# A two-layer expert FFN with modulated LayerNorm on one core: group sums kept in SBUF, x loaded three items ahead, y accumulated onto a negative mean, and 1/std as a power on GpSimd

## What is computed

```
h = gelu(einsum('btel,elf->btef', xr, W1) + b1)      # 8 groups, 128 -> 512
y = einsum('btef,efl->btel', h, W2) + b2             # 512 -> 128, then [B, T, 1024]
scale, shift = split(silu(emb) @ emb_W + emb_b)      # one row for each of the 4 batches
hn = layernorm(y, ln_g, ln_b) * (1 + scale) + shift  # over the 1024 columns
out = x + silu(hn) @ out_W + out_b                   # 1024 x 1024
```

## Time and profile before

| | us |
|---|---|
| median of 3 runs (lowest, highest) | 740.33 (739.93, 741.41) |
| profiled execution, own time | 743.72 |
| its span, first to last instruction | 741.7 |
| busy in the span: PE, DVE, ACT, POOL | 693.2, 602.8, 488.9, 172.7 |
| granted TensorE clock, mean | 0.979 |

### The profile page before, as it was taken

One profiled execution on the slowest core, in us unless ns is written; L12 is line 12 of the kernel. 1 busy time (PEld: TensorE's weight loads), 2 busy tenths in 40 slices (PEclk: granted clock), 3 DMA queues, 4 the chain that ended last, 5 costly groups with the idle time before them and its releaser, 6 DMA issues.

```text
span 741.7 us, 8277 instructions
## 1 busy us (share of the span) xinstructions
PE 693.2 (93%) x2960; PEld 541.6 (73%) x2960; DVE 602.8 (81%) x663; ACT 488.9 (66%) x566; POOL 172.7 (23%) x116
## 2 busy tenths in 40 slices
PE   9999989999899997999998299999999999999998
PEld 6887577767677776767776188777777778777887
DVE  6866469687868767979886299999999999999952
ACT  6886567778777857786889066555566665666510
...
GB/s 173 268 360 300 178 98 173 209 209 204 188 200 209 102 330 194 147 117 154 153 166 284 304 234 202 202 207 213 228 228 212 217 216 218 203 218 179 184 156 57
DMA packets 76120, 150.07 MB, mean 202 GB/s; under 512 B 12704, under 2 KB 50080, under 8 KB 72240
## 3 DMA queue, kind: packets, MB, share of 16 engines
...
q10 hardware_dynamic: 8352, 0.10, 0.6%
...
...
## 4 chain that ended last, share of the span: by engine, by line
DVE 34%; PE 27%; DMA 16%; issue 13%; ACT 9%; SPq 1%; DVEq 0%; POOL 0%; ACTq 0%; POOLq 0%
PE psum L1028 11%; PE psum L1006 8%; PE psum L988 7%; DMA xT_raw<-in_xT 5%; DVE res L852 5%; DMA y_sum<-y_stage 4%; ACT g_raw L514 4%; DVE yb L760 4%; DMA o_raw<-in_out_W 3%; DVE yb L782 3%; DVE d_lo L813 3%; DVE g_lo L728 3%; DVE a_lo L806 3%; DMA res<-out_b_all 2%; ACT g_hi L520 2%
## 5 line engine op out<-in xcount | busy, mean ns | idle before, releaser
L728 DVE TENSOR_TENSOR g_lo<-g_raw,g_hi 128x1024 fp32r<-128x1024 f32 x128 | 159.2, 1250 | 83.1 <-ACT g_hi L520 80.5
L514 ACT ACTIVATE g_raw<-psum,cols 128x1024 f32<-128x1024 f32 x128 | 142.6, 1114 | 42.9 <-DVE g_lo L728 24.3
L988 PE MATMUL psum<-xT_hi,W 128*128 128x512 f32 x508 | 139.8, 397 | 10.5 <-ACT g_raw L514 10.4
L1006 PE MATMUL psum<-g_hi,W 128*128 128x512 f32 x512 | 139.9, 395 | 5.8 <-DVE g_hi L726 3.3
L1028 PE MATMUL psum<-wa,d_hi 128*128 128x512 f32 x512 | 128.6, 394 | 17.8 <-DVE res L852 17.8
L1028 PEld LDWEIGHTS psum<-wa,d_hi 128*128 128x128 f32 x512 | 97.5, 191 | 38.7 <-issue 18.2
L988 PEld LDWEIGHTS psum<-xT_hi,W 128*128 128x128 f32 x508 | 95.3, 190 | 37.3 <-ACT g_raw L514 16.1
L1006 PEld LDWEIGHTS psum<-g_hi,W 128*128 128x128 f32 x512 | 96.5, 190 | 29.2 <-DVE g_hi L726 5.5
L852 DVE TENSOR_TENSOR res<-psum,res 128x512 f32<-128x512 f32 (+1 forms) x113 | 76.3, 675 | 37.3 <-PE psum L1028 20.9
L557 ACT ACTIVATE yb<-yb,mod_c,mod_a 128x256 f32<-128x256 f32 x120 | 62.4, 591 | 50.3 <-DVE yb L782 50.3
L444 POOL PARTITION_ALL_REDUCE var_all<-var_total x16 | 43.6, 2723 | 211.6 <-DVE var_total L773 211.6
...
## 6 DMA issues: line engine op xcount, KB each, us to landing
y_scratch<-y_stage SPq DMA_DIRECT2D x32, 512.0 KB, 3.1
y_sum<-y_stage POOLq DMA_DIRECT2D x32, 512.0 KB, 8.4
yb<-y_scratch SPq DMA_DIRECT2D x16, 1024.0 KB, 6.4
res<-in_x SPq DMA_DIRECT2D x32, 512.0 KB, 4.1
res<-out_b_all POOLq DMA_DIRECT2D x32, 512.0 KB, 5.9
xT_raw<-in_xT SPq DMA_DIRECT2D x31, 512.0 KB, 5.5
out<-res SPq DMA_DIRECT2D x31, 512.0 KB, 5.5
emb_raw<-in_emb_W SPq DMA_DIRECT2D x8, 1024.0 KB, 9.7
```

The costliest lines, as they stand in the source:

```text
L514: nc.scalar.activation(g_raw[:, m % 2], ring(m), ACT.Gelu, bias=cols[:, R_B1 + k:R_B1 + k + 1]).then_inc(gelu_done, 1)
L728: nc.vector.tensor_tensor(g_lo[:, m % 2], g_raw[:, m % 2], g_hi[:, m % 2].bitcast(F32), ALU.subtract).then_inc(glo_done, 1)
L988: mm = nc.tensor.matmul(ring(m)[:, half], W[:, g % WS, w, cut], v[:, n % 2, half], start=(k == 0), stop=(k == 2))
L1006: mm = nc.tensor.matmul(y_psum(n)[:, half], W[:, g % WS, w, cut], v[:, m % 2, half], start=(c == 0 and k == 0), stop=(c == C - 1 and k == 2))
```

## The change

The sums over groups of items 0 to 19 are held in SBUF (`y_acc`): items of group 0 are staged into it, and items 4 to 19 are added by VectorE (the new `add_y` there) at the third chunk of the next item. Only items 20 to 31 still add in DRAM. x is loaded one item earlier. The prepared weights and `res` are loaded in another order and the two first `add_bias` are issued before the last item's `add_y`. For pairs from 2 on `centre` is gone: ScalarE writes minus the mean into `yb` (`prefill`), and GpSimd's queue brings y with an accumulating DMA. `root`, its table loads and `invert` are gone: GpSimd computes var/D + eps and raises it to -0.5, in place in `var_all`. The items at which weights are converted move. The diff, cut to its core:

```diff
-    W_ITEM = {1: 1, 2: 3, 3: 5, 4: 7, 5: 10, 6: 13, 7: 17}
+    W_ITEM = {1: 1, 2: 3, 3: 5, 4: 9, 5: 12, 6: 13, 7: 17}
     W_AT = {n: g for g, n in W_ITEM.items()}
-    O_ITEM = {0: 8, 1: 11, 2: 14, 3: 18}
+    O_ITEM = {0: 6, 1: 10, 2: 14, 3: 18}
     O_AT = {n: g for g, n in O_ITEM.items()}
 
-    O_STEP = {(0, 0): (0, 1), (0, 2): (2, 3), (1, 0): (4, 5), (1, 2): (6,)}
-    VISIT = 6
+    O_STEP = {0: (0, 1), 3: (2, 3), 4: (4, 5), 7: (6,)}
+    VISIT = 5
+
+
+
+    ADD_ITEMS = list(range(NT, HG * NT + G - HG))
+    ADD_NO = {n: k + 1 for k, n in enumerate(ADD_ITEMS)}
+    DRAM_ITEMS = list(range(HG * NT + G - HG, N))
 
...
+    y_sum = nc.dram_tensor("y_sum", [NT, P, TA], F32, kind="Internal").ap()
...
+        y_acc = [at(f"y_acc{t}", [P, TA], R0 + o * KB) for t, o in enumerate((126, 0, 4, 130))]
...
-        res = at("res", [P, 4, D], R0 + 48 * KB)
...
+        res = at("res", [P, 4, D], R0 + 16 * KB)
...
-        t3 = [at(f"t3_{k}", [P, HG, BANK], R0 + o * KB, F32R) for k, o in enumerate((72, 64))]
-        b22 = [at(f"b22_{k}", [P, HG, BANK], R0 + o * KB, F32R) for k, o in enumerate((40, 88))]
-        t4 = [at(f"t4_{k}", [P, HG, BANK], R0 + o * KB, F32R) for k, o in enumerate((96, 80))]
+        t3 = [at(f"t3_{k}", [P, HG, BANK], R0 + o * KB, F32R) for k, o in enumerate((32, 72))]
+        b22 = [at(f"b22_{k}", [P, HG, BANK], R0 + o * KB, F32R) for k, o in enumerate((40, 80))]
+        t4 = [at(f"t4_{k}", [P, HG, BANK], R0 + o * KB, F32R) for k, o in enumerate((96, 88))]
...
+        def y_loads(p):
+
+            return (p - 2) // 3 + 1
+
         def raw_count(g):
...
             def load_sum(p):
-                if p >= 1:
+                if p > 3:
                     sp.wait_ge(mean_done, p)
-                sp.dma_start(sum_in[:], y_sum[p]).then_inc(sum_landed, 16)
+                sp.dma_start(sum_in[:], y_sum[p // PT, :, p % PT * TP:(p % PT + 1) * TP]).then_inc(sum_landed, 16)
 
...
+            def store_y(n):
+                sp.wait_ge(y_staged, n + 1)
+                g, t = ORDER[n]
+                sp.dma_start(y_scratch[PT * t:PT * t + PT, :, g].rearrange("h p t -> p h t"),
+                             staged_in(n).rearrange("p (h t) -> p h t", h=PT)).then_inc(y_stored[n % 2], 16)
+
+            def store_sum(t, n):
+                sp.wait_ge(y_added, ADD_NO[n])
+                sp.dma_start(y_sum[t], y_acc[t][:]).then_inc(sum_stored[t], 16)
+
             load_x(1)
             load_w(1)
+            sp.wait_ge(xlo_done, 1)
+            load_x(2)
             for n in range(N):
-                if n + 2 < N:
-                    sp.wait_ge(xlo_done, n + 1)
-                    load_x(n + 2)
+                if n + 3 < N:
+                    sp.wait_ge(xlo_done, n + 2)
+                    load_x(n + 3)
                 if n == 0:
                     sp.wait_ge(w_split, 2)
                     load_w(2)
...
+                if n - 3 in O_AT:
+                    g = O_AT[n - 3]
...
                     if g + 1 < HG:
                         sp.wait_ge(o_sum, 4 * (g + 1))
                         load_o(g + 1)
+                if HG * NT - NT + 2 <= n <= HG * NT:
+                    t = n - (HG * NT - NT + 1)
+                    store_sum(t, n - 1)
                 if n == Y0_ITEM + 1:
                     for s in range(2):
                         sp.wait_ge(y_stored[s], 16 * len(range(s, Y0_ITEM + 1, 2)))
+                    for t in (1, 2):
+                        sp.wait_ge(sum_stored[t], 16)
                     load_y(0)
-                    load_y(2)
-                    sp.wait_ge(y_summed[0], 16 * sums_before(Y0_ITEM))
-                    load_sum(0)
                 if n == Y0_ITEM + 2:
                     sp.wait_ge(o_split, 7 * HG)
                     load_y(1)
-                    load_sum(1)
-                if n == Y0_ITEM + 4:
-                    load_sum(2)
-                if n == Y0_ITEM + 9:
+                    store_sum(0, Y0_ITEM)
+                if n == Y0_ITEM + 8:
+                    sp.wait_ge(sum_stored[0], 16)
                     load_sum(3)
...
-                if n == N - 2:
-                    sp.wait_ge(xlo_done, N)
-                    for q in range(2):
+                if n in (N - 3, N - 2):
+                    sp.wait_ge(s2_done, C * n)
+                    for q in (0, 1) if n == N - 3 else (2, 3):
                         load_res(q)
                 if n == N - 1:
-                    sp.wait_ge(s1_done, M)
-                    load_wc(C_T3, LO, t3)
-                    for q in range(2, 4):
-                        load_res(q)
+                    sp.wait_ge(s2_done, C * n)
+                    load_wc(C_T3, HI, t3)
                 if n < N - 1:
-                    sp.wait_ge(y_staged, n + 1)
-                    g, t = ORDER[n]
-                    sp.dma_start(y_scratch[PT * t:PT * t + PT, :, g].rearrange("h p t -> p h t"),
-                                 y_stage[:, n % 2].rearrange("p (h t) -> p h t", h=PT)).then_inc(y_stored[n % 2], 16)
+                    store_y(n)
 
             sp.wait_ge(glo_done, M)
-            load_wc(C_T3, HI, t3)
+            load_wc(C_T3, LO, t3)
             sp.wait_ge(s2_done, M)
             load_wc(C_B22, HI, b22)
             load_wc(C_B22, LO, b22)
             load_wc(C_T4, LO, t4)
...
-            sp.wait_ge(dlo_done, 1)
-            sp.wait_ge(alo_done, 1)
-            load_y(3)
+            store_y(N - 1)
             for s in range(2):
                 sp.wait_ge(y_stored[s], 16 * (N // 2))
-            for t in range(NT):
-                sp.wait_ge(y_summed[t], 16 * G)
+            sp.wait_ge(y_summed[NT - 1], 16 * (G - HG))
             load_wc(C_T4, HI, t4)
+            load_sum(4)
             for p in range(NP):
-                if 1 <= p and p + 3 < NP:
-                    load_sum(p + 3)
-                    sp.wait_ge(s_sum, 4 * (p + 1))
-                    load_y(p + 3)
+                if 1 <= p and p + 4 < NP:
+                    load_sum(p + 4)
                 if p >= 1:
                     sp.wait_ge(added, 7 * (p - 1) + P3)
...
-                if k == 0:
-                    pool.dma_start(place, part).then_inc(y_summed[t], 16)
+                if dram_sums(n) == 1:
+                    pool.wait_ge(sum_stored[t], 16)
                 else:
-                    pool.wait_ge(y_summed[t], 16 * k)
-                    pool.dma_start(place, part, accum_op=ALU.add).then_inc(y_summed[t], 16)
+                    pool.wait_ge(y_summed[t], 16 * (dram_sums(n) - 1))
+                pool.dma_start(y_sum[t], y_stage[:, n % 2], accum_op=ALU.add).then_inc(y_summed[t], 16)
...
             def mean_of(p):
-                pool.wait_ge(sum_landed, 16 * (p + 1))
-                if p >= 1:
+                if p < 3:
+                    pool.wait_ge(y_added, ADD_NO[Y0_ITEM])
+                else:
+                    pool.wait_ge(sum_landed, 16 * (p - 2))
+                if 1 <= p <= 2:
                     pool.wait_ge(centred, 2 * p)
-                nc.gpsimd.partition_all_reduce(mean_all[:], sum_in[:], P, bass.bass_isa.ReduceOp.add
-                                               ).then_inc(mean_done, 1)
+                elif p > 2:
+                    pool.wait_ge(prefilled, 2 * (p - 2))
+                total = y_acc[0][:, p * TP:(p + 1) * TP] if p < 3 else sum_in[:]
+                nc.gpsimd.partition_all_reduce(mean_all[:], total, P, bass.bass_isa.ReduceOp.add).then_inc(mean_done, 1)
+
+            def load_y(p):
+
+                pool.wait_ge(prefilled, 2 * (p - 1))
+                pool.dma_start(yb[p % 3][:], y_scratch[p], accum_op=ALU.add).then_inc(y_landed[p % 3], 16)
 
             def var_of(p):
                 pool.wait_ge(var_tree, 3 * p + 3)
                 if p >= 2:
-                    pool.wait_ge(std_done, p - 1)
+                    pool.wait_ge(normed, 2 * (p - 1))
                 nc.gpsimd.partition_all_reduce(var_all[:, p % 2], var_total[:], P, bass.bass_isa.ReduceOp.add
                                                ).then_inc(var_done, 1)
+                pool.wait_ge(var_done, p + 1)
+                nc.gpsimd.tensor_scalar(var_all[:, p % 2], var_all[:, p % 2], 1.0 / D, LN_EPS, ALU.mult, ALU.add
+                                        ).then_inc(std_done, 1)
+                pool.wait_ge(std_done, p + 1)
+                nc.gpsimd.tensor_tensor(var_all[:, p % 2], var_all[:, p % 2], power[:].to_broadcast([P, TP]), ALU.pow
+                                        ).then_inc(rstd_done, 1)
 
...
+            pool.wait_ge(power_set, 1)
             for n in range(N):
...
                     var_of(0)
+                    mean_of(2)
                 if n == Y0_ITEM + 5:
-                    mean_of(2)
                     var_of(1)
+                    load_y(2)
                 if n == Y0_ITEM + 10:
                     mean_of(3)
-                add_y(n)
-            pool.wait_ge(out_b_landed, 16)
-            for q in range(2):
```

(73 more changed lines are left out.)

93 lines of the change are left out of this document (37 added, 56 removed).

## The result

The changed kernel takes 1518.69 us (median of 4 runs, 1516.99 to 1519.70) where the kernel before took 740.47 in the runs beside it (739.93 to 741.41): 2.05 times as long, interval 2.047 to 2.054. The forecast was 726, and the range ended at 778. The profiled execution's own time is 1519.70 and its span 1518.0, at a mean granted clock of 0.734.

A forecast was written before the change was run, and what follows sets the result against it. Late x was taken to bound the first half, VectorE the pairs. From 741.7 us, items gave -16.5, the passage -8 and the pairs' ring +10: span 727.2, profiled execution 729.2, median 726; range 701 to 778.

The forecast's parts named there:

- the price of the power: GpSimd's power on 128x256, once a pair: 0.70 us as any tensor_tensor, 0.80 with gaps; 2.69 taken from above.
- the power is long: Rival, pairs: a power of about 1.9 us or more makes the kernel slower; at 2.7, median 761; power or load long, 0.35.
- the ring: Pairs: waits from all-reduce through power, y's load, squares, silu and VectorE take 21.1 us a pair, 10 us more over 12 pairs.
- items 6 to 20: 14 middle items of the first half: 10 of their 23 us lost are gained, with VectorE busy 149.4 us.
- items 20 to 31: Last 11 items of the first half: 6 of 10.6 us gained, as VectorE and ScalarE lose work and x is on time.
- passage, item 31 to P4's add: Between the halves: weights and res loaded earlier gain 8 us, between 3 and 15.
- items 0 to 6: Early items of the first half: 0.5 us gained.
- wait for t4's high part: Passage: TensorE stalls 9 us for t4's high part, which can't be issued before item 31's stores have landed.
- load of y, accumulating: Pairs: the 1 MB accumulating load on GpSimd's queue takes 7.4 us, within 6.4 to 8.4.
- the third rival: First half: VectorE's idle time stays and 17 us of adds come on top; median between 736 and 749; chance 0.14.
- The first rival: Pairs: with a load of 5.3 us or less the ring doesn't bind, TensorE's 19.04 rules; median 701; chance 0.11.
- signs named beforehand: Trace signs: right if y's DMA is issued right behind the power; wrong if a power row is over 2 us.

The follow-up runs named there:

- e3: The changed kernel with GpSimd's power replaced by a multiplication of the same shape and order (result not 1/std): 872.77 us, one run.
- e8: The kernel before with a GpSimd multiplication and powers of several sizes appended after its last work, each waiting for the one ahead: 892.57 us, one run.
- e4: The kernel before plus one tiny GpSimd tensor_scalar on 128x4 behind each variance all-reduce of the second half: 911.90 us, one run.
- e1: The changed kernel with GpSimd's tensor_scalar and power taken out, root on ScalarE and reciprocal on VectorE back: 721.15 us, 0.971 of the kernel before.
- e5: e1 with the load of y for pair p+3 issued ahead of the variance all-reduce for p+2 on GpSimd: 714.92 us, 0.963 of the kernel before.

## Why the prediction was wrong

**The step that failed** is the price of the power: "The price of the power is what no row shows." and, three sentences on, "I take the low value, because it is the same instruction on the same engine." It is 41.2 us, over fifty times the 0.80 in the sum. A product in that place is 0.62 (e3), and e8 shows on the same shape that the operation decides. The row taken for the upper bound bounded nothing: an all-reduce and a power have only the engine and the shape in common. The prediction had said that every us of the power costs 12; with that slope an unmeasured price leaves no forecast to make from its lower end. The rival "the power is long" had the mechanism, the place and the point of 1.9 us from which it decides, and a chance of 0.35, but its size stopped at 2.7, and the range at 4.1, with 0.13 left for longer ones. The Trainium skill (GPSIMD Engine Reference, Elementwise) has about 12 cycles an element for a body that branches on data, the estimate of 2.6 us in the prediction. It doesn't agree: measured is 0.16 us an element, at the 1.2 GHz used for that estimate 193 cycles.

**Not in the sum at all** was GpSimd's switch between all-reduce and elementwise work: 7.2 us in the ring and another 4.0 through the late bias. Together they would have turned the sign without any power, as e3 shows (872.8 us). A row of it was there: the first tensor_tensor of the kernel before waits 10.1 us for "issue", as the earlier trace rows has at its end, the only such wait on GpSimd above 1 us, and its MODIFY_POOL_CONFIG is at 95.8. That kernel's only other change, to the all-reduce, starts at 260.0 and is hidden, because GpSimd waits for the sum until 278.03; from there on it runs only all-reduces and DMA issues. The Trainium skill (GPSIMD Engine Reference, Instruction dispatch) says that the first call to a freshly loaded kernel pays an instruction load of approximately 6 us "with no visible profile instruction". The size agrees with the 5.8 to 6.2 us before 12 of the 13 all-reduces that follow a change in e4's second half; the 6.8 to 8.9 us before an elementwise instruction are longer. The page speaks of a first call only, but with a MODIFY_POOL_CONFIG at each change every round of these kernels has two.

**The other steps**, measured on e1 and on the changed kernel:

| step | forecast | measured |
|---|---|---|
| items 6 to 20 | -10 us; VectorE busy 149.4 | -14.0; 149.40 |
| items 20 to 31 | -6 | -6.2 |
| items 0 to 6 | -0.5 | +4.6 |
| passage, item 31 to P4's add | -8 (3 to 15 gained) | -2.4 |
| wait for t4's high part | 9 | 9.44 |
| first add in the passage | no wait | 1.66 for out_b, 3.4 for TensorE |
| load of y, accumulating | 7.4 (6.4 to 8.4) | 8.0 to 8.6 in the pairs, once 9.1 |
| e1's pair (forecast with e1) | 20.2 | 19.9 |
| ring of the change, its other terms | 21.1 | 73.07 less the four differences: 20.8 |

The middle items gained more than "a bit under half" of their loss: with x there, the idle time of VectorE fell from 43 to 12 us, so the third rival, which let it stay, is wrong. The loss in the first six items wasn't foreseen, and its cause wasn't tried. The traces place it: up to item 4 e1 gains 2.6 us, and from item 4 to 6 it takes 35.0 us where the kernel before takes 27.8. There the condition product comes an item earlier and out_W's first block two, and TensorE stands for 3.5 us before 85.24.

The passage missed its bounds. The prediction's sum for it was off by itself: waits of 1.5, 9 and 2 us where 17.8 were leave 5.3 and not 8. And that the wait for t4's high part came out at 9.44 is luck. TensorE wanted it 20.9 us after item 31's eviction, where 16 was forecast, and it was there after 30.4, where 25 was forecast: both ends are 5 us late. The store that it waits for took 23.9 us (issued at 386.22, t4 issued behind it at 410.15) and so landed 25.5 us after item 31, not 18.

In e1 VectorE's relief is worth 0.4 us a pair and no more, since y's load closes the ring as the prediction said; e5, which only shortens the ring, gets the rest.

The first rival, that the ring doesn't bind, is false for the change and for e1: it needed a load of 5.3 us or less, and the load takes 8. What spoke for it, that the rows were timed with the DMA engines 78% busy, doesn't count: with them 23% busy in the changed kernel's pairs the load takes 8.05 to 8.6 us, as in e1, where they are 88% busy. The Trainium skill's formula (DMA: Bandwidth & Descriptors, Anatomy of one DMA) gives an estimate of 4.4 for 1 MB; the accumulating loads here don't agree with it.

Two of the signs named beforehand tell it at a glance: the power row over 2 us, and the DMA of y issued right behind it.
